# A graph attention layer on one core: an addition ahead of z, a multiplication ahead of the message, u ahead of z on TensorE, and another wait for the gathers

## What is computed

```python
hl = x @ Wl.T + bl
hr = x @ Wr.T + br
s = (take(hl, src) + take(hr, dst)) * alpha            # alpha: edge_attr_128, one row per edge
s = where(s >= 0, s, 0.2 * s)
smax = segment_max(s, dst)
e = exp(s - take(smax, dst))
att = e / take(segment_sum(e, dst), dst)
y = segment_sum(take(x, src) * att, dst)
out = layernorm(x + y)
```

## Time and profile before

| | us |
|---|---|
| median of three runs | 1437.57 |
| the three runs | 1435.41, 1437.57, 1439.32 |
| span of the profiled execution, first to last instruction | 1129.4 |
| VectorE busy in the span | 1072.6 (95%) |
| TensorE busy in the span | 1079.0 (96%) |
| ScalarE busy in the span | 998.6 (88%) |
| GpSimd busy in the span | 820.7 (73%) |

### The profile page before, as it was taken

One profiled execution on the slowest core, in us unless ns is written; L12 is line 12 of the kernel. 1 busy time (PEld: TensorE's weight loads), 2 busy tenths in 40 slices (PEclk: granted clock), 3 DMA queues, 4 the chain that ended last, 5 costly groups with the idle time before them and its releaser, 6 DMA issues.

```text
span 1129.4 us, 34988 instructions
## 1 busy us (share of the span) xinstructions
PE 1079.0 (96%) x9403; PEld 1014.7 (90%) x9403; DVE 1072.6 (95%) x1526; ACT 998.6 (88%) x2606; POOL 820.7 (73%) x858
## 2 busy tenths in 40 slices
PE   6879999999999999999999999999999999999984
PEld 5779999999999999999999999999999899999863
DVE  7889999999999999999999999999999999999967
ACT  4359999999999999999999999999999889998996
POOL 5577777777777777777777777777777777777770
PEclk9889999999999999999999999999999999999997
DMA  9887776666667776767766666677676666676533
GB/s 227 290 221 191 192 187 191 190 188 188 191 187 191 189 189 187 192 189 190 189 189 188 189 191 190 188 189 188 191 189 185 186 188 182 187 191 183 143 99 114
DMA packets 231064, 211.97 MB, mean 188 GB/s; under 512 B 46375, under 2 KB 204286, under 8 KB 230788
## 3 DMA queue, kind: packets, MB, share of 16 engines
q0 software_dynamic: 39872, 108.39, 35.5%
q1 hardware_dynamic: 190442, 100.03, 32.4%
q10 hardware_dynamic: 565, 1.33, 0.4%
HBM read 198.95 MB, written 11.47 MB: 186 GB/s over the span
## 4 chain that ended last, share of the span: by engine, by line
PE 51%; POOL 26%; issue 11%; ACT 3%; DVE 2%; DMA 0%; ACTq 0%; POOLq 0%; DVEq 0%
POOL xg L435 25%; PE ps_w L654 19%; PE ps_sT L590 11%; PE ps_u L630 9%; PE ps_z L608 5%; PE ps_q L599 2%; PE ps_u L636 2%; PE ps_qT L618 2%; ACT attr L853 1%; DVE stats L1161 1%; ACT acc L802 0%; DMA xg<-gather_rows,srcT 0%; ACT right L811 0%; DVE acc L1086 0%; ACT ex L749 0%
## 5 line engine op out<-in xcount | busy, mean ns | idle before, releaser
L435 POOL DMA_INDIRECT xg<-gather_rows,srcT x808 | 764.9, 947 | 253.0 <-issue 235.9
L654 PE MATMUL ps_w<-onehot,ex 128*128 128x128 f32 x3328 | 405.7, 275 | 1.2 <-ACT acc L806 1.2
L654 PEld LDWEIGHTS ps_w<-onehot,ex 128*128 128x128 f32 x3328 | 388.4, 192 | 1.8 <-issue 1.6
L1095 DVE TENSOR_TENSOR_SCAN ps_F<-line,B,ps_sT 128x512 f32<-128x512 bf16 x208 | 266.1, 1279 | 1.0 <-issue 1.0
L1100 DVE TENSOR_TENSOR_SCAN B<-line,ps_F 128x512 f32<-128x512 bf16 x208 | 254.0, 1221 | 7.2
L630 PEld LDWEIGHTS ps_u<-right,onehotT 128*128 128x128 f32 x1664 | 208.5, 192 | 18.9 <-issue 0.2
L630 PE MATMUL ps_u<-right,onehotT 128*128 x1664 | 221.1, 276 | 0.0
L802 ACT ACTIVATE acc<-ps_w 128x768 f32 x208 | 168.7, 811 | 23.5
L1105 DVE TENSOR_TENSOR z<-ps_sT,B 128x512 f32<-128x512 f32 x208 | 143.9, 692 | 7.1
L1121 DVE TENSOR_TENSOR ex<-ps_z,xg 128x512 f32<-128x512 f32 x208 | 141.7, 681 | 5.7 <-ACT ps_z L773 5.7
L1129 DVE TENSOR_TENSOR v<-ps_u,attr 128x512 f32<-128x512 f32 x208 | 141.8, 682 | 0.3
(11 more groups left out here) (264 smaller groups left out, 1164.1 us busy)
## 6 DMA issues: line engine op xcount, KB each, us to landing
attr<-edge_attr_in SPq DMA_DIRECT2D x832, 64.0 KB
line<-step_lines SPq DMA_DIRECT2D x182, 128.0 KB
xg<-gather_rows,srcT POOLq DMA_INDIRECT x808
gather_rows<-acc SPq DMA_DIRECT2D x12, 512.0 KB, 6.0
line<-soon_lines SPq DMA_DIRECT2D x26, 128.0 KB
edge<-step_lines SPq DMA_DIRECT2D x182, 4.0 KB
acc<-x_in SPq DMA_DIRECT2D x6, 448.0 KB, 7.6
xg<-x_in SPq DMA_DIRECT2D x6, 448.0 KB, 5.6
```

The costliest lines, as they stand in the source:

```text
L435: pool.indirect_dma_start(out=xg[:, k % SLOTS, i, :], out_offset=None, in_=rows_dram, in_offset=bass.IndirectOffsetOnAxis(ap=srcT[:, k * W ...
L654: last = nc.tensor.matmul(columns, ex[:, (k - 1) % 2, c, i, :], onehot[:, (k - 1) % 3, i, :], start=(i == 0), stop=(i == WIDE - 1), skip_g ...
L1095: V.tensor_tensor_scan(ps_F[:, :], line[:, k % LINES, 0:GE], ps_sT[:, :], B[:, (k - 1) % 3, GE - 1:GE], ALU.add, ALU.max).then_inc(F_ok, 1)
```

## The change

On GpSimd the gathers' wait for the transposes of z (`z_ps`) becomes a wait for v (`v_ok`) of the step after. On TensorE the distances and the transposes of z move from their place behind s to a place behind u, and change places with one another. On VectorE the addition moves ahead of z, and v ahead of the message.

```diff
@@ gpsimd, in the loop over k @@
                 lead = max(LEAD, SLOTS - 1 - k // 40)
                 if k >= lead:
-                    pool.wait_ge(z_ps, k - lead + 1)
+                    pool.wait_ge(v_ok, k - lead + 2)
@@ tensor, body(k) @@
                     last.then_inc(sT_ps, 1)
-                if has(k):
-                    j = k % EDGES
-                    if k >= 1:
-                        pe.wait_ge(oh_ok, k)
-                    for i in range(WIDE):
-                        last = nc.tensor.matmul(ps_q[:, i * P:(i + 1) * P], edge[:, j, i * P:(i + 1) * P], node[:, :],
-                                                start=(i == 0), stop=(i == WIDE - 1), skip_group_check=True)
-                    last.then_inc(q_ps, 1)
-                    pe.wait_ge(z_ok, k + 1)
-                    if k == 0:
-                        pe.wait_ge(src_sb, 2)
-                    if k >= 1:
-                        pe.wait_ge(msg_ok, k)
-                    for i in range(WIDE):
-                        last = nc.tensor.transpose(ps_z[:, i * D:(i + 1) * D], z[:, k % 2, i * P:(i + 1) * P], ident[:, :])
-                    last.then_inc(z_ps, 1)
                 if has(k + 4):
...
                     last.then_inc(u_ps, 1)
+                if has(k):
+                    pe.wait_ge(z_ok, k + 1)
+                    if k == 0:
+                        pe.wait_ge(src_sb, 2)
+                    if k >= 1:
+                        pe.wait_ge(msg_ok, k)
+                    for i in range(WIDE):
+                        last = nc.tensor.transpose(ps_z[:, i * D:(i + 1) * D], z[:, k % 2, i * P:(i + 1) * P], ident[:, :])
+                    last.then_inc(z_ps, 1)
+                    j = k % EDGES
+                    if k >= 1:
+                        pe.wait_ge(oh_ok, k)
+                    for i in range(WIDE):
+                        last = nc.tensor.matmul(ps_q[:, i * P:(i + 1) * P], edge[:, j, i * P:(i + 1) * P], node[:, :],
+                                                start=(i == 0), stop=(i == WIDE - 1), skip_group_check=True)
+                    last.then_inc(q_ps, 1)
@@ vector, body(k) @@
                                          ALU.add, ALU.max).then_inc(B_ok, 1)
-                    dve.wait_ge(B_ok, k + 1)
-                    if k >= 2:
-                        dve.wait_ge(z_ps, k - 1)
-                    V.tensor_tensor(z[:, k % 2, :], ps_sT[:, :], B[:, k % 3, :], ALU.subtract).then_inc(z_ok, 1)
                 if has(k + 2):
...
+                if has(k):
+                    dve.wait_ge(B_ok, k + 1)
+                    if k >= 2:
+                        dve.wait_ge(z_ps, k - 1)
+                    V.tensor_tensor(z[:, k % 2, :], ps_sT[:, :], B[:, k % 3, :], ALU.subtract).then_inc(z_ok, 1)
+                if has(k + 2):
+                    j = (k + 2) % ATTRS
+                    dve.wait_ge(attr_in[j], 64 * ((k + 2) // ATTRS + 1))
+                    dve.wait_ge(h_ok, k + 3)
+                    if k >= 0:
+                        dve.wait_ge(sT_ps, k + 1)
+                    V.tensor_tensor(v[:, k % 2, :, :], u_of(ps_u), attr[:, j, :, :], ALU.mult).then_inc(v_ok, 1)
                 if k == STEPS:
                     ratio(0)
                 if has(k - 1):
...
-                if has(k + 2):
-                    j = (k + 2) % ATTRS
-                    dve.wait_ge(attr_in[j], 64 * ((k + 2) // ATTRS + 1))
-                    dve.wait_ge(h_ok, k + 3)
-                    if k >= 0:
-                        dve.wait_ge(sT_ps, k + 1)
-                    V.tensor_tensor(v[:, k % 2, :, :], u_of(ps_u), attr[:, j, :, :], ALU.mult).then_inc(v_ok, 1)
```

## The result

The changed kernel takes 1784.11 us (median of four runs, 1777.67 to 1797.42). Timed beside it, the kernel before takes 1438.44 (four runs, 1435.41 to 1439.35). The ratio is 1.2433, 95% interval 1.2376 to 1.249: 24% slower, where I forecast 0.6% and a range that ended at 1454. The profiled execution took 1787.38 us with a span of 1785.6.

What follows compares the result with a forecast made beforehand. Bound: compute step (4.84 us, VectorE and TensorE tied) first, GpSimd's gathers (5.00) at the end; after the change, a 4.915 us chain. Middle +6.8, start +0.9, end +0.5: 1437.6 + 8.2 = 1445.8 us, range 1435.5 to 1454.

Steps and rivals of the forecast that it cites:

- outside of anything the profile shows; I carry it unchanged: Whole run: the median 1437.57 us exceeds the profiled span by 308.2 us, added unchanged to the forecast.
- It costs nothing, and its loosening brings nothing: GpSimd's gather wait: charged 25 times, 7.6 us, 0.30 each, the normal issue time; changing it gives no gain.
- All three rivals: Whole kernel: no overlap behind the scan, 1469 us (8%); not slower, 1437 (14%); busiest engines set time, 1415 (3%).
- The chain: Loop first scan, second scan, z, s, next first scan: 4.56 us plus 0.36 gives 4.92, taken as 4.915 a step.
- the overlap behind the scan: VectorE, addition behind the second scan: starting before the scan's span is over saves 0.11 us a step.
- rival (1): VectorE, behind the second scan: addition starts 0.03 us after it, nothing saved, step 5.03, time 1469 us; 8%.
- The sum: Whole run: middle +6.8 us, start +0.9, end +0.5, together +8.2 us.
- VectorE's multiplication ahead of the message, "nothing": VectorE: v comes 0.7 us earlier, the message later with its exponential still long over; no time gained or lost.
- Hidden, thinly: TensorE's u ahead of z's transposes: ScalarE's 2.53 us behind them ends at 9.2, before the next distances at 9.5.
- If that cover goes: Next distances, u, z's transposes and ScalarE's 2.53 us: a chain under 4.8 us, still no bound.
- Rival (3): All engines: those with highest busy shares set the time; 0.11 us less per step brings 23 us, 1415; 3%.

Runs made afterwards that it cites:

- e3: Only the gathers' wait changed (v of the step after instead of z's transposes), against the kernel before, chip 3: 1132.57 us, ratio 0.9998.
- e7: Only the gathers' wait changed (v of the step after instead of z's transposes), against the kernel before, chip 15: 1814.14 us, ratio 1.2601.
- e5: VectorE's and TensorE's new orders with the gathers' old wait, against the kernel before, chip 14: 1491.01 us, ratio 1.0369.
- e13: Kernel before with its old gather wait checked only every second step, one step later, letting eight gathers go at once, chip 15: 1988.62 us, ratio 1.3791.
- e12: The whole changed kernel, against the kernel before, on chip 7: 1136.23 us against 1131.45, ratio 1.0042.
- e0: The kernel before, unchanged, timed and profiled again on chip 3: 1132.48 us, ratio 1.0002, span 1129.2.
- e1: Only VectorE's new order (addition ahead of z, v ahead of the message), against the kernel before, chip 3: 1136.58 us, ratio 1.0038.
- e2: Only TensorE's new order (distances and z's transposes behind u), against the kernel before, chip 3: 1150.83 us, ratio 1.016.
- e4: The whole changed kernel again, against the kernel before, on chip 14: 1782.06 us, ratio 1.2401.
- e6: The kernel before, unchanged, timed and profiled on chip 15: 1440.24 us, span 1438.4.
- e14: Kernel before with one wait added: a step's third gather waits for z of the next step, chip 15: 1510.42 us, ratio 1.0491.
- e8: The whole changed kernel, against the kernel before, on chip 15: 1790.46 us, ratio 1.2403.
- e16: Kernel before with only two of four gathers per step from the eleventh on, chip 12: 1122.05 us, ratio 0.9916.

## Why the prediction was wrong, and where it was right

**The step that failed: "outside of anything the profile shows; I carry it unchanged".** The span of the profiled execution was 308.2 us under the median of the runs, and I took this for a constant. It was the mark of another chip: wherever an execution's time and span were both seen, on either kind of chip, they differ by 1.8 us (1.75 to 1.88). The timed runs belonged to a kernel whose step is 6.32 us and not the 4.84 of the earlier trace rows, one that waits 331 us for z's transposes. My whole working is about the other one. Had I read it as "the profile is not of these runs", no number could have followed from it, but the range should have been far wider, and I would have had to ask which wait could be worth 1.5 us a step. That the changed kernel came out slower, as forecast, is luck on such a chip: its 346 us come from a cause that the forecast doesn't have.

**"It costs nothing, and its loosening brings nothing" (the gathers' wait).** Right where the profile was taken (e3: 0.9998), wrong where the time was: 1.26 on the chip of e7. The wait was a brake: it kept GpSimd's runs at four gathers. Of the 24%, 3.7 are there with both orders and the old wait (e5), and the rest comes with the new wait; that the loss comes by joined runs is supported by e13, which makes runs of eight with the old semaphore and loses 38%. All three rivals of the prediction kept the same assumption, so none reaches the result.

**The chain: right in its mechanism, 0.02 us too long.** On a chip that holds nothing (e12, above) each term is seen. Scan to scan 1.32 as said; second scan to addition 1.14 as said; z's start to the end of s, 605.03 to 606.93, 1.90 as said; s to the next scan 0.09 as said. Only the addition's start to z's was 0.44 instead of 0.47, as the addition takes 0.54 us there instead of 0.56. Sum 4.89, measured 4.894, predicted 4.915. That sum contains the overlap behind the scan, so rival (1) is out: the addition starts 0.08 before the scan's span is over (603.45 + 1.22 = 604.67). I had given as a rule of the Trainium skill's page "VectorE: DVE Perf Modes", section "The DRAIN you can't avoid", that the next instruction starts only when the pipe is empty. The same section adds that a next instruction that isn't held starts earlier, and the 0.08 agrees with that; with that sentence the section gives rival (1) no support.

**The sum, on such chips.** Against e0: from first scan to scan 4, 19.88 and 21.06, +1.2 (predicted +0.9). Scan 4 to 205, 981.00 and 983.86, +2.9 (predicted +6.8, as 987.9: the 0.02 a step too much is the 4.0 us between 987.9 and 983.86). From scan 205 to the end, 61.80 and 62.28, +0.5 (predicted +0.5). In all +4.5, with 0.6 more before the first scan, where nothing was changed; the runs give +4.8 (e12) against the +8.2 forecast. The charge of 7.4 us in e0 for additions that wait for gathers is gone in e12, as said, and the last gather ends at 1068.53, as said, but 6 us ahead of the last addition (1074.50) and not 9, since the steps are shorter.

**VectorE's multiplication ahead of the message, "nothing", and TensorE's order, "Hidden, thinly"**: right as far as both come together (e1 and e12 cost the same, 1.0038 and 1.0042). I had looked for the cover in ScalarE's 2.53 us. The nearer one is u behind v: with v where it was, it costs 18.8 us (e2). That v's new place is worth this was not in the prediction. "If that cover goes" it put a chain under 4.8 us and "still no bound"; the loop through u and v in e2 is 4.955 a step.

**Rival (3)**, by which the busiest engine sets the time, fell: VectorE's own work shrank, as the 0.11 us of VectorE idle in front of the scan in e12 shows, and the kernel became slower on both kinds of chip.

## What to carry over

Compare the profiled execution's own time with the timed runs first: if they differ by more than the few us that every run shows around its span, the profile is of another chip's execution, and no sum made in it can be carried over. Ask of a wait that costs nothing what it keeps from happening; this one kept GpSimd's runs at four gathers, and on a chip of 1438 us that was worth 20% (e4 against e5) to 26% (e7). When two edits come together, cost each without the other too: one may be the other's cover.

## What the runs showed of the hardware

- The kernel before takes 1131 to 1132 us on chips 3, 7 and 12, and 1438 to 1440 on chips 14 and 15: 27% apart for the same program, with the medians within 0.2% on each kind. Chip 15 was timed twice, 25 minutes apart, at 1440.12 and 1438.91. No chip was seen to change from one kind to the other; that it is a lasting state and not the chip itself isn't excluded.
- On chips 14 and 15 TensorE's semaphores come late while GpSimd issues indirect gathers every 1.25 us: 1.0 to 1.4 us after a run of four (e6, e14), 1.8 to 2.2 after a run of eight (the late s of e7, e8 and e13), and in e13 up to 8.3 us after the last matmul of s. Sums that ended 1.0 to 2.5 us into a run of two were heard of at once (0.12 us, 57 of 57, e14); news was late there only where the pause before the run was 0.63 to 0.72 us (3 times). On chips 3, 7 and 12 runs of some 800 gathers delay nothing. TensorE's own instructions are slowed as well late in a run: in the changed kernel from 616.55 to 619.38 single matmuls and weight loads start 0.7 us apart instead of 0.11.
- Why these chips do so, from which moment of a run the hold begins (in e14 sums that end 1.5 to 2.0 us into a run of four are late, in the changed kernel s at that place mostly isn't), and how long a pause must be for each semaphore, stays open. GpSimd's issuing as the cause rests on the late semaphores' place behind the runs' ends and on e13 and e14, which move with the runs; no run without gathers, or with half of them, was made on such a chip.
- No version that does the whole work beat the kernel before on either kind of chip; with half the gathers left out (e16) it is 0.8% faster on chip 12.
